# A two-layer adapter kernel: another order in its opening, in its pairs' steps and in its queues

## What is computed

```
x: (64, 64, 1024) float32; 64 batches of 64 tokens
layer 0:  y = einsum('bct,bcd->bdt', x, W0[id0])            # a 64x64 matrix chosen per batch
          x = x + ffn0(y)      # router (8 experts, best 2), rank-16 LoRA experts A, Bm, scaling 0.5
layer 1:  y = einsum('bij,bkj->bik', x, W1[id1])            # a 1024x1024 matrix chosen per batch
          x = x + base_w(y) + base_b + 0.5 * delta(y)       # router (16 experts, best 2), rank-64 LoRA
```

## Time and profile before

| | |
|---|---|
| median of 3 runs | 1194.68 us (1187.48 to 1197.7) |
| the profiled execution | 1188.06 us, its span 1186.5 us |
| TensorE busy | 1109.9 us, 94% |
| VectorE busy | 689.2 us, 58% |
| ACT busy | 506.3 us, 43% |
| TensorE's granted clock, mean | 0.981 of full |

### The profile page before, as it was taken

The page is one execution under the profiler, slowest core; times in us unless marked ns, Lnnn a source line. Parts: engine busy times, 40 slices in busy tenths (PEclk is TensorE's granted clock), DMA queues, the critical chain, the costliest instruction groups (busy, mean ns, idle before and its releaser), DMA issues.

```text
span 1186.5 us, 22134 instructions
## 1 busy us (share of the span) xinstructions
PE 1109.9 (94%) x5799; PEld 915.7 (77%) x5800; DVE 689.2 (58%) x1310; ACT 506.3 (43%) x1019; POOL 221.2 (19%) x354
## 2 busy tenths in 40 slices
PE   4799969989999899999999999999999999999998
PEld 4799958867888687777887778766666778888886
DVE  4688953573554728364555386834444366556666
ACT  1112213563644628363556362134445344444443
POOL 1111200020110202010111000054544142312210
PEclk9899979999999999999999999999999999999999
DMA  5399873484573928476665432168888899999995
GB/s 208 112 331 336 272 281 107 131 312 138 196 256 103 332 78 297 154 243 209 218 218 177 152 101 82 60 208 321 324 318 325 304 405 366 333 352 335 317 330 200
DMA packets 113773, 283.11 MB, mean 239 GB/s; under 512 B 17074, under 2 KB 22194, under 8 KB 111794
## 3 DMA queue, kind: packets, MB, share of 16 engines
q1 hardware_dynamic: 84192, 178.96, 42.9%
q0 software_dynamic: 29216, 102.91, 25.4%
q10 hardware_dynamic: 306, 0.53, 0.2%
HBM read 181.65 MB, written 100.70 MB: 238 GB/s over the span
## 4 chain that ended last, share of the span: by engine, by line
PE 73%; DVE 11%; issue 6%; DMA 5%; ACT 3%; DVEq 1%; SPq 1%; POOL 0%; ACTq 0%; POOLq 0%
PE psum L1412 17%; PE psum L1414 16%; PE psum L1413 16%; PE psum L1610 4%; PE psum L1611 3%; PE psum L1507 3%; PE psum L1499 2%; PE psum L1619 2%; DVE x1g L1022 2%; PE psum L1525 2%; PE psum L1527 2%; PE psum L1508 2%; PE psum L1422 1%; DMA rawb<-baseT 1%; ACT w L802 1%
## 5 line engine op out<-in xcount | busy, mean ns | idle before, releaser
L1412 PE MATMUL psum<-base_hi,xp_hi 128*128 128x512 f32 x512 | 204.8, 400 | 3.4 <-ACT nat L793 1.5
L1414 PE MATMUL psum<-base_hi,xp_lo 128*128 128x512 f32 x512 | 200.5, 392 | 0.0
L1413 PE MATMUL psum<-base_lo,xp_hi 128*128 128x512 f32 x512 | 200.3, 391 | 0.0
L1412 PE MATMUL psum<-w,xp_hi 128*128 128x512 f32 x448 | 184.7, 412 | 15.4 <-issue 8.6
L1414 PE MATMUL psum<-w,xp_lo 128*128 128x512 f32 x448 | 179.2, 400 | 0.0
L1413 PE MATMUL psum<-w,xp_hi 128*128 128x512 f32 x448 | 178.9, 399 | 0.0
L625 POOL DMA_DIRECT2D raw<-w1T x112 | 59.2, 528 | 450.0 <-DVE w L1053 447.4
L1053 DVE TENSOR_TENSOR w<-raw,w 128x1024 fp32r<-128x1024 f32 x112 | 132.4, 1217 | 6.2 <-ACT w L737 4.4
L784 ACT ACTIVATE xp_hi<-xp 128x256 fp32r<-128x256 f32 x124 | 51.4, 417 | 183.8 <-PE psum L1414 156.2
L1152 DVE TENSOR_TENSOR xp_lo<-xp,xp_hi 128x256 fp32r<-128x256 f32 x124 | 51.8, 424 | 122.2 <-ACT xp_hi L784 101.2
L1412 PEld LDWEIGHTS psum<-base_hi,xp_hi 128*128 128x128 f32 x512 | 96.4, 188 | 28.5 <-issue 3.8
(11 more groups left out here) (273 smaller groups left out, 1935.6 us busy)
## 6 DMA issues: line engine op xcount, KB each, us to landing
raw<-w1T POOLq DMA_DIRECT2D x120, 512.0 KB, 5.6
delta_scratch<-dl SPq DMA_DIRECT2D x80, 512.0 KB
xp<-act_scratch SPq DMA_DIRECT2D x74, 256.0 KB, 2.9
act_scratch<-yT SPq DMA_DIRECT2D x72, 256.0 KB, 5.1
act_scratch<-x1g SPq DMA_DIRECT2D x16, 1024.0 KB, 5.6
x1t<-act_scratch SPq DMA_DIRECT2D x64, 256.0 KB
out<-x1t SPq DMA_DIRECT2D x62, 256.0 KB
xg<-xT SPq DMA_DIRECT2D x15, 1024.0 KB, 8.4
```

The lines of the kernel that those rows point to most:

```text
L1412: mm(out, a_hi, b_hi, start=start, stop=False, skip_group_check=True)
L1413: mm(out, a_hi, b_lo, start=False, stop=False, skip_group_check=True)
L1414: return mm(out, a_lo, b_hi, start=False, stop=stop, skip_group_check=True)
```

## The change

- Opening: the two loads of id1 are issued by ACT, no longer ahead of SP's loads; ACT's w0tab loads wait for xg's first half. Index work is reordered: TensorE does `index_sums(2)` ahead of `first_z(0)`, VectorE does `index_3` behind `hidden_low(0)` and `index_4` behind the first group's step, TensorE `index_sums(4)` between groups 0 and 1.
- Between the layers: TensorE no longer waits for the last x1 additions of the first layer (the wait for the first pair's `xp_lo` remains, which stands behind them on VectorE). POOL waits for all x1g stores before it loads the second adapter's weights.
- Pairs: `base_w` is split in 16 halves of a chunk (128x512), in steps 0 to 15, through two staging halves, at the end of a step. `y_turned` on ACT makes both `yq_hi` passes first and both `yT` passes after, each of these behind VectorE's `yq_lo` of its bank; VectorE's `yq_lo` waits for `yq_hi` instead of `yT`. `y_copy` stands ahead of the second half of `x_high` and `x_low`. `rh_of` comes behind the seventh chunk, `rh_part` and `rh_sum` behind the last weight chunks.
- SP: iteration j loads pair j+2 and a base half and then stores pair j-1, not j.

```diff
@@ -46,2 +46,3 @@
 HALF = D // 2
+PARTS = 2 * KC
 
@@ -173,3 +174,3 @@
             yq_lo = sb(s, "yq_lo", [P, KC, P], F32R)
-            rawb = sb(s, "rawb", [P, D])
+            rawb = sb(s, "rawb", [P, 2, HALF])
             rhl = sb(s, "rhl", [P, Z2])
@@ -391,4 +392,2 @@
 
-            sp.dma_start(id_i, id1.rearrange("(b a) -> b a", a=1)).then_inc(id1_in, 16)
-            sp.dma_start(id_row_i, id1.partition_broadcast(NW)).then_inc(id1_in, 16)
             for q in range(2):
@@ -446,4 +445,9 @@
             load_pair(1)
-            sp.dma_start(rawb[:, :], baseT[0, :, :]).then_inc(rawb_in, 16)
-            with sp.Fori(0, total) as j:
+            sp.dma_start(rawb[:, 0, :], baseT[0, :, 0:HALF]).then_inc(rawb_in, 16)
+            sp.wait_ge(xp_lo_done, 2)
+            sp.wait_ge(xp_in, 32)
+            load_pair(2)
+            sp.wait_ge(rawb_in, 16)
+            sp.dma_start(rawb[:, 1, :], baseT[0, :, HALF:D]).then_inc(rawb_in, 16)
+            with sp.Fori(1, total) as j:
                 sp.wait_ge(xp_lo_done, 2 * j + 2)
@@ -452,7 +456,11 @@
                 load_pair(j + 2)
-                with sp.If(j < KC - 1):
-                    chunk = baseT[bass.ds(nc.s_assert_within(j + 1, 1, KC - 1), 1), :, :].rearrange("a p d -> p (a d)")
-                    sp.wait_ge(base_lo_done, j + 2)
-                    sp.dma_start(rawb[:, :], chunk).then_inc(rawb_in, 16)
-                store_pair(j)
+                with sp.If(j < PARTS - 1):
+                    n = nc.s_assert_within(j + 1, 2, PARTS - 1)
+                    part = baseT[bass.ds(n // 2, 1), :, bass.ds(n % 2 * HALF, HALF)].rearrange("a p d -> p (a d)")
+                    home = rawb[:, bass.ds(n % 2, 1), :].rearrange("p a d -> p (a d)")
+                    sp.wait_ge(rawb_in, j * 16 + 16)
+                    sp.wait_ge(base_lo_done, j + 1)
+                    sp.dma_start(home, part).then_inc(rawb_in, 16)
+                store_pair(j - 1)
+            store_pair(total - 1)
 
@@ -620,2 +628,4 @@
                                x1s[bass.ds(b, 1), :, :].rearrange("b p (i c) -> p (b i) c", c=C)).then_inc(xp_first, 16)
+            for s in range(2):
+                pool.wait_ge(x1_out[s], 16 + 16 * (NG // 2))
             with pool.Fori(1, used + 1) as u:
@@ -651,6 +661,9 @@
         def _(act):
+            act.dma_start(id_i, id1.rearrange("(b a) -> b a", a=1)).then_inc(id1_in, 16)
+            act.dma_start(id_row_i, id1.partition_broadcast(NW)).then_inc(id1_in, 16)
             act.dma_start(ids0[0:1, :], id0.rearrange("(a b) -> a b", a=1)).then_inc(w0_in, 16)
+            act.dma_start(rbias[:, :], rb0.partition_broadcast(P)).then_inc(rbias_in, 16)
+            act.wait_ge(xg_first[0], 16)
             for h in range(2):
                 act.dma_start(w0tab[h * C:(h + 1) * C, :], w0).then_inc(w0_in, 16)
-            act.dma_start(rbias[:, :], rb0.partition_broadcast(P)).then_inc(rbias_in, 16)
 
@@ -704,21 +717,25 @@
 
-            def y_turned(v, half):
-
-                ks = slice(half * KC // 2, (half + 1) * KC // 2)
-                src = bank(half)
-                act.wait_ge(yT_done, 2 * v + half + 1)
-                if half == 0:
-                    act.wait_ge(rh_done, v + 1)
-                act.activation(yq_hi[:, ks, :], src.rearrange("p (i r) -> p i r", r=P), ACT.Copy
-                               ).then_inc(yq_hi_done, 1)
-                if half == 0:
-                    act.wait_ge(yT_out, 32 * v + 32)
-                act.activation(yT[:, :, ks, :].rearrange("p b i c -> p i b c"),
-                               src.rearrange("p (i b c) -> p i b c", b=2, c=C), ACT.Copy).then_inc(yT_ready, 1)
+            def y_turned(v):
+                for half in range(2):
+                    ks = slice(half * KC // 2, (half + 1) * KC // 2)
+                    act.wait_ge(yT_done, 2 * v + half + 1)
+                    if half == 0:
+                        act.wait_ge(rh_done, v + 1)
+                    act.activation(yq_hi[:, ks, :], bank(half).rearrange("p (i r) -> p i r", r=P), ACT.Copy
+                                   ).then_inc(yq_hi_done, 1)
+                act.wait_ge(yT_out, 32 * v + 32)
+                for half in range(2):
+                    ks = slice(half * KC // 2, (half + 1) * KC // 2)
+                    act.wait_ge(yq_lo_done, 2 * v + half + 2)
+                    act.activation(yT[:, :, ks, :].rearrange("p b i c -> p i b c"),
+                                   bank(half).rearrange("p (i b c) -> p i b c", b=2, c=C), ACT.Copy
+                                   ).then_inc(yT_ready, 1)
 
             def base_high(j):
-                with act.If(j < KC):
-                    chunk = base_hi[:, bass.ds(nc.s_assert_within(j, 0, KC - 1), 1), :].rearrange("p a d -> p (a d)")
+                with act.If(j < PARTS):
+                    n = nc.s_assert_within(j, 0, PARTS - 1)
+                    part = base_hi[:, :, :].rearrange("p k d -> p (k d)")[:, bass.ds(n * HALF, HALF)]
+                    home = rawb[:, bass.ds(n % 2, 1), :].rearrange("p a d -> p (a d)")
                     act.wait_ge(rawb_in, 16 * j + 16)
-                    act.activation(chunk, rawb[:, :], ACT.Copy).then_inc(base_hi_done, 1)
+                    act.activation(part, home, ACT.Copy).then_inc(base_hi_done, 1)
 
@@ -739,6 +756,4 @@
                 w_chunks(range(2))
-                y_turned(j, 0)
-                y_turned(j, 1)
+                y_turned(j)
                 w_chunks(range(2, KC // 2))
-                base_high(j)
                 act.wait_ge(mm_done, KC * j + KC // 2)
@@ -746,5 +761,3 @@
                 w_chunks(range(KC // 2, LATE))
-                rh_part(j)
                 act.wait_ge(mm_done, KC * j + KC)
-                x_high(j + 1, 1)
                 with act.If(j == lone):
@@ -753,3 +766,6 @@
                     y_copy(j, False)
+                x_high(j + 1, 1)
                 w_chunks(range(LATE, KC))
+                rh_part(j)
+                base_high(j)
 
@@ -771,4 +787,3 @@
                         step(j, lone)
-            y_turned(total, 0)
-            y_turned(total, 1)
+            y_turned(total)
 
@@ -1036,6 +1051,4 @@
             index_2()
-            index_3()
             dve.wait_ge(rbias_in, 16)
             gates0(0)
-            index_4()
             dve.wait_ge(const_split_hi, 1)
@@ -1043,4 +1056,7 @@
             hidden_low(0)
+            index_3()
             for s in range(RING):
                 step0(s, s)
+                if s == 0:
+                    index_4()
             dve.wait_ge(const_split_hi, 2)
@@ -1088,3 +1104,3 @@
                 ks = slice(half * KC // 2, (half + 1) * KC // 2)
-                dve.wait_ge(yT_ready, 2 * v + half + 2)
+                dve.wait_ge(yq_hi_done, 2 * v + half + 1)
                 tt(yq_lo[:, ks, :], bank(half).rearrange("p (i r) -> p i r", r=P), yq_hi[:, ks, :].bitcast(F32),
@@ -1093,8 +1109,9 @@
             def base_low(j):
-                with dve.If(j < KC):
-                    i = bass.ds(nc.s_assert_within(j, 0, KC - 1), 1)
+                with dve.If(j < PARTS):
+                    n = nc.s_assert_within(j, 0, PARTS - 1)
+                    low, high = (b[:, :, :].rearrange("p k d -> p (k d)")[:, bass.ds(n * HALF, HALF)]
+                                 for b in (base_lo, base_hi))
+                    home = rawb[:, bass.ds(n % 2, 1), :].rearrange("p a d -> p (a d)")
                     dve.wait_ge(base_hi_done, j + 1)
-                    tt(base_lo[:, i, :].rearrange("p a d -> p (a d)"), rawb[:, :],
-                       base_hi[:, i, :].rearrange("p a d -> p (a d)").bitcast(F32), ALU.subtract
-                       ).then_inc(base_lo_done, 1)
+                    tt(low, home, high.bitcast(F32), ALU.subtract).then_inc(base_lo_done, 1)
 
@@ -1117,3 +1134,2 @@
                 low_chunks(range(2, KC // 2))
-                base_low(j)
                 one = alone(dve, j + 1)
@@ -1121,4 +1137,2 @@
                 low_chunks(range(KC // 2, LATE))
-                rh_sum(j)
-                x_low(j + 1, 1, one)
                 with dve.If(j == lone):
@@ -1127,3 +1141,6 @@
                     y_copy(j, False)
+                x_low(j + 1, 1, one)
                 low_chunks(range(LATE, KC))
+                rh_sum(j)
+                base_low(j)
 
@@ -1457,3 +1474,2 @@
                 if isinstance(g, int) and g == 0:
-                    index_sums(4)
                     pe.wait_ge(const_split, 1)
@@ -1472,4 +1488,4 @@
             index_sums(1)
-            first_z(0)
             index_sums(2)
+            first_z(0)
             first_z(1)
@@ -1480,2 +1496,4 @@
                 group0(s, s)
+                if s == 0:
+                    index_sums(4)
             with pe.Fori(1, NG // RING - 1) as t:
@@ -1486,4 +1504,2 @@
                 group0(NG - RING + s, s, last_group=s == RING - 1)
-            pe.wait_ge(x1_added, 4 * NG)
-
 
@@ -1531,3 +1547,3 @@
                         turn(j)
```

(6 more changed lines are left out.)

## The result

The change makes the kernel about 1% faster: 1180.59 us (median of 6 runs) against 1193.21 (6 runs beside it), ratio 0.990 (0.9868 to 0.9931). Forecast was 1168, with a range of 1154 to 1183. The direction was right and the size about half of what was forecast: 12.6 us came where 25.2 were expected against the same median, and 26.7 against 1194.68, the median that the forecast had.

The account below looks back on a forecast made before the run. It took VectorE beside TensorE to bound the first layer and TensorE at 2.4 GHz an undisturbed pair, with waits elsewhere. 8.5 + 3.5 + 9.4 - 1.5 + 1.1 = 21.0 off 1188.06 gave 1167.1, forecast as 1168, range 1154 to 1183.

Parts of the forecast that it names:

- part 4: Pairs, yp first and yT last: half pairs minus 1.5 us, last half pair's follower gains 1.1; net loss 0.4.
- Part 3: Pairs, base in halves at a step's end: the two long steps lose their excess, 9.4 us gained.
- Part 2: Change of layers: faster x1g store and no TensorE wait for x1_added gain 3.5 us; held-back weight loads cost nothing.
- Part 1: Opening: first group's products 13 us sooner, 4.5 paid back for index_4; net gain 8.5 us.
- Rival (b): Opening: w0tab lands late beside the xg loads, so the gain is 4.5 us, not 8.5: 1172; chance 0.13.
- my bound of 10.5: Opening: upper bound of its gain in us, if TensorE keeps 2.4 GHz through it.
- (a): Half pairs: VectorE has slack and turn waits really go, 10 us gained instead of 0.4 lost: 1157; chance 0.17.
- (c): Adapter-changing steps: ACT's new yq_lo wait and lost clock cost 32 us against 21 gained: 1199; chance 0.07.
- Rival (d): Pairs: raw loads crowd the DMA engines, ACT waits for xp or raw, Part 3 gains half: 1180; chance 0.13.
- "rh behind the seventh chunk ... free": Pairs: moving rh behind the seventh chunk keeps the same 16 matmuls and was put at no cost.

Follow-up runs that it names:

- before with base part (7): Kernel before with only base in 16 halves at a step's end, two staging halves and SP's new load/store order: 1183.45 us, ratio 0.992.
- before with y_copy first (6): Kernel before with only y_copy moved ahead of the second half of x_high and x_low: 1185.33 us, ratio 0.9941.
- before with y_turned (5): Kernel before with only the new y_turned order (both yq_hi, then both yT behind yq_lo): 1203.78 us, ratio 1.0098.
- after with old y_turned (2): Changed kernel with y_turned as before (yq_hi and yT bank by bank, yq_lo waiting for yT): 1163.69 us, ratio 0.9757.
- after with yT late (4): Changed kernel with both yT passes and their yq_lo wait behind w chunks 2 and 3 and x_high's first half: 1163.16 us, ratio 0.9754.
- 8 with rh sixth (12): On experiment 8, rh_of back behind the sixth chunk, rh_part and rh_sum ahead of the last weight passes: 1170.64 us, ratio 0.9806.
- experiment 10: Kernel before with only the change of layers (no TensorE wait for x1_added, POOL waiting for all x1g stores): 1191.05 us, ratio 0.9983.
- experiment 8: Changed kernel with both yT passes late and the old order of the first loads, index order still new: 1160.01 us, ratio 0.9719.
- experiment 1: Kernel before timed and profiled again, no edit: 1193.57 us, ratio 1.001.

## Why the prediction was off, point by point

**First, from where the sum was taken off.** The 21.0 us were subtracted from the profiled execution, 1188.06, which was 5.2 us quicker than the median of its kernel, 1193.21, and only 0.9 was put back. So 4.2 of the 12.6 us between 1168 and 1180.59 are no part's fault. The other 8.4 are: the parts were to gain 21.0 and gained 12.6. By themselves, in medians, base gained 9.3 (forecast 9.4), the opening 4.5 (8.5) and the change of layers 2.0 (3.5), the last with an interval that holds 0. If the parts add, which no run shows, part 4 lost 3.2 where 0.4 was forecast.

The pairs' steps, summed from the profiles (us), show which part did what. All other steps are in the last column only:

| kernel | five half pairs and the interval after each | the two half pairs in a row | the two base steps | all 36 |
|---|---|---|---|---|
| before | 131.54 | 41.64 | 37.30 | 502.28 |
| before with base part (7) | 130.70 | 44.05 | 28.65 | 495.46 |
| before with y_copy first (6) | 127.98 | 41.76 | 36.90 | 497.97 |
| before with y_turned (5) | 137.63 | 42.13 | 37.11 | 512.11 |
| after | 137.05 | 43.47 | 28.24 | 502.99 |
| after with old y_turned (2) | 124.92 | 40.45 | 28.24 | 485.67 |
| after with yT late (4) | 124.96 | 39.50 | 28.24 | 483.77 |
| 8 with rh sixth (12) | 126.58 | 43.67 | 29.26 | 491.18 |

- **Part 3, base: right**, 9.4 forecast, 9.1 in the profile and 9.3 by itself.
- **Part 2, change of layers: right in place and size (3.5 against 3.2 in the profile), wrong in what I called free.** I said that the held-back weight loads cost nothing because their own use is far off. What they cost others, I did not ask. With base at its old place the first pair took 5.9 us more (experiment 10); in the changed kernel it does not.
- **Part 1, the opening: mis-sized**, 8.5 forecast, 3.0 to 4.5 measured. Rival (b) happened: w0tab first used at 18.32. It had 0.13. I had the fourth copy "exactly in time", which took for granted that a load behind some 4.6 MB of SP's that were still to land takes as long as one ahead of them. The rest of the walk was right: where w0tab comes first again (experiment 8), y_of(0) is at 16.87 and 16.8 was forecast. The smaller part was index_4: I charged 4.5 us, and took the idle that it makes without the clock behind it, though my bound of 10.5 names the clock: TensorE ran at 1.2 GHz from 48 to 52 us (0.50), and the second and third group lost 6.3.
- **Part 4 is the step that failed**, in the walk through a half pair: "So the sum ends where it did, and 0.96 gained at the turn is lost at the pair's end." The chain was in the text: ACT stands for yq_lo (1.5 forecast, 1.74 measured), VectorE for w 2 (1.1 and 1.61). It was priced as if what stands behind it had slack up to the sum. It hasn't: the first half of xp_lo of the next pair, which y_copy first does nothing for, comes 1.7 us later, TensorE stands 1.79 us for it, in three of four places runs at a lower clock behind it, and the next turn comes 14.36 instead of 11.96 us after the last. The sum itself ended 13.3 us after the turn, where it had been 11.9. That wait costs 17 us of the changed kernel (experiments 2 and 4), where the sum let it eat up no more than the 0.96 us a half pair that the turn gained.
- **How much part 4 lost as a whole is less sure.** In the profiles it is 9.8 us (502.99 against 493.2, which is 502.28 less the 9.1 of the base steps), or 7.5 against experiment 7's own 495.46; by the medians above 3.2. The two profiles lie 8.3 us off the medians together, which is enough for the difference. That it isn't further from the 0.4 that was forecast is luck: by the medians a loss of 17 and gains of some 14 stand in it, and the sum had neither at its size.
- **I charged only the seven half pairs.** The six full steps that change adapter have the same queue: together they take 89.0 us, with the old y_turned 87.1 and with yT late 86.0.
- **Rivals (a) and (c) were both at work.** y_copy first gained 7.4 us by itself (experiment 6), where (a) said 10. Once y_turned is out of its way, and with rh behind the seventh chunk, half pair and follower fall from 26.3 to 25.0 us each (131.54 to 124.92 over five). (c) had the right place, and its price of 32 us was too high; y_turned costs 17 us in the changed kernel and 11 in the kernel before. I weighed the two as alternatives for one sum, when they are two terms of opposite sign.
- **Rival (d) did not happen.** Over the pairs of the changed kernel ACT has no wait for rawb left, and its waits for xp fall from 53.6 us in 13 times to 4.5 in one.
- **"rh behind the seventh chunk ... free"** was a term put at nothing that is worth something: up to 10 us once yp is early (experiment 12), since it gives VectorE one more chunk's time for yq_lo.
- A slip that changes nothing: the turn after 261.21 follows after 18.48 us, not 18.59.

What stays open: whether the parts add, what in the opening holds w0tab up (SP's loads or the small ones of its own queue), and whether the few us of spread between executions (experiment 1) have one cause.

## What to carry to other kernels

A wait on an engine that takes its work in order is priced by what is queued behind it, followed until the first engine that has no slack, and the lost clock after that stop belongs in the price. When two passes of one engine must wait for another's pass, put the work that the other is going to need ahead of them: here that one move was worth 17 us. And a transfer that is held back is not free because its own use is late; ask which load it will now meet. And take the sum off the median, not off one execution.

## What the runs showed of the hardware

- The place of an issue counted for more than its time. w0tab (two loads of 256 KB on ACT's queue) was first used at 7.69 us when it was issued from 1.54, ahead of xg and of rbias; at 17.17 when issued from 3.18, behind them; and at 18.32 when issued from 7.10, with some 4.6 MB of SP's loads still to land. The Trainium skill, DMA: Bandwidth & Descriptors, section "Issuing engines are not separate DMA queues", says that DMAs of all issuing engines run on the same 16 DMA engines and interleave there. These runs agree: another queue gave w0tab no lane of its own, yet, issued at 7.10, it was in use at 18.32, while SP's load of 1 MB issued at 4.74 landed at 21.23.
- An idle of 1.79 us before 502.25 was followed by a granted clock of 0.70 over the next 4 us, the same idle before 447.17 by 1.00, and the idles of 0.96 us in the kernel before by 1.00 (501 to 517 us); one of 3.75 us before 47.22 was followed by 0.50. So idles of under 2 us can cost the clock, and need not.
